# A row transposition for the expert tiles, moved from TensorE to VectorE in 32x32 pieces

## The reference

```
f    = layernorm(x)
rho  = tanh(ctx @ Ws + f @ W + b) . w             # every token against 77 context rows
att  = softmax(masked rho);  t = att @ ctx
x    = x + tanh(g0) * (tanh(t @ Wcw') * f + tanh(t @ Wcb'))
n    = layernorm(x)
top2 of softmax(n @ router')                      # 2 of 8 experts for each token
x    = x + tanh(g1) * sum over experts e of  weight_e * (gelu(n @ w1[e]') @ w2[e]')
```

## Time and profile before

| | us |
|---|---|
| median of three runs | 578.42 |
| the profiled execution | 579.2 |
| its span, first to last instruction | 577.1 |
| PE busy | 518.5 (90%) |
| DVE busy | 355.9 (62%) |
| ACT busy | 354.0 (61%) |
| POOL busy | 112.1 (19%) |

### The profile page before, as it was taken

The page is one execution under the profiler, slowest core; times in us unless marked ns, Lnnn a source line. Parts: engine busy times, 40 slices in busy tenths (PEclk is TensorE's granted clock), DMA queues, the critical chain, the costliest instruction groups (busy, mean ns, idle before and its releaser), DMA issues.

```text
span 577.1 us, 10197 instructions
## 1 busy us (share of the span) xinstructions
PE 518.5 (90%) x3432; PEld 334.1 (58%) x3433; DVE 355.9 (62%) x1176; ACT 354.0 (61%) x314; POOL 112.1 (19%) x96
## 2 busy tenths in 40 slices
PE   7887979667799878989979999999999999999993
PEld 5432323102255434545534555788899999999993
DVE  4889998899984899995799985375111111111110
ACT  1678999989999998999989997231111111111110
POOL 2000000050001161201251111145322122212222
PEclk9688989777899999999999999999999999999998
DMA  4101960045422046233237443359666666665541
GB/s 130 38 0 26 384 257 0 1 151 185 155 76 82 10 152 193 56 120 105 70 109 208 140 136 101 93 155 271 213 184 184 182 182 182 182 182 182 173 98 21
DMA packets 32831, 77.47 MB, mean 134 GB/s; under 512 B 4471, under 2 KB 25591, under 8 KB 26647
## 3 DMA queue, kind: packets, MB, share of 16 engines
q1 hardware_dynamic: 24848, 67.22, 34.2%
q0 software_dynamic: 7344, 9.72, 9.3%
q10 hardware_dynamic: 599, 0.02, 0.1%
HBM read 60.65 MB, written 16.29 MB: 133 GB/s over the span
## 4 chain that ended last, share of the span: by engine, by line
PE 59%; DVE 22%; ACT 13%; DMA 3%; issue 2%; POOL 0%; SPq 0%; DVEq 0%; POOLq 0%
PE h_ps L713 20%; PE y_bank L725 20%; PE rho L678 13%; DVE hbuf L884 11%; ACT hbuf L566 8%; ACT hbuf L572 3%; PE misc L658 3%; PE xsT_bank L667 2%; PE xsT_bank L701 1%; DMA xs<-row_scratch 1%; DMA hgT<-in_x 1%; ACT hgT L595 1%; DMA out<-y_sb,meta 1%; DVE rows L943 1%; DVE stats L851 1%
## 5 line engine op out<-in xcount | busy, mean ns | idle before, releaser
L566 ACT ACTIVATE hbuf<-hbuf 128x2048 f32<-128x2048 f32 (+2 forms) x160 | 247.2, 1593 | 33.0 <-DVE hbuf L884 32.3
L884 DVE TENSOR_SCALAR hbuf<-featT,txtb 128x512 f32<-128x512 f32 x525 | 216.1, 480 | 19.7 <-PE rho L678 18.6
L678 PE MATMUL rho<-hbuf,wpad 128*32 128x512 f32 x1232 | 175.3, 649 | 37.3 <-ACT hbuf L572 26.4
L713 PEld LDWEIGHTS h_ps<-xsT,w_st 128*128 128x128 f32 x1280 | 148.9, 192 | 28.3 <-issue 26.0
L713 PE MATMUL h_ps<-xsT,w_st 128*128 128x128 f32 x1280 | 154.8, 277 | 2.2 <-issue 1.4
L725 PE MATMUL y_bank<-w_sb,hgT 128*128 x640 | 149.7, 384 | 1.7 <-DVE y_sb L1056 1.7
L595 ACT ACTIVATE hgT<-h_ps 128x1024 f32<-128x1024 f32 x40 | 40.7, 1019 | 163.2 <-PE h_ps L713 163.1
L725 PEld LDWEIGHTS y_bank<-w_sb,hgT 128*128 128x128 f32 x640 | 117.4, 190 | 36.3 <-issue 22.5
L510 POOL DMA_INDIRECT out<-y_sb,meta x40 | 66.3, 1657 | 300.1 <-DVE y_sb L1056 160.9
L678 PEld LDWEIGHTS rho<-hbuf,wpad 128*32 128x32 f32 x1232 | 30.1, 113 | 124.2 <-ACT hbuf L572 54.6
L1042 DVE COPY xsT<-xsT_bank 128x256 f32<-128x256 f32 x40 | 16.9, 422 | 81.6 <-PE xsT_bank L701 81.6
(11 more groups left out here) (131 smaller groups left out, 189.4 us busy)
## 6 DMA issues: line engine op xcount, KB each, us to landing
w_st<-in_w SPq DMA_DIRECT2D x40, 1024.0 KB, 4.9
w_sb<-in_w SPq DMA_DIRECT2D x8, 1024.0 KB, 14.0
xs<-row_scratch SPq DMA_DIRECT2D x40, 132.5 KB, 4.7
row_scratch<-pad SPq DMA_DIRECT2D x33, 132.5 KB, 21.6
x_res<-in_x SPq DMA_DIRECT2D x4, 512.0 KB, 5.9
out<-x_res SPq DMA_DIRECT2D x4, 512.0 KB, 3.5
hgT<-in_x SPq DMA_DIRECT2D x3, 512.0 KB, 3.6
out<-y_sb,meta POOLq DMA_INDIRECT x40, 6.3
```

What stands on the lines that cost most here:

```text
L566: ins = s.activation(h, h, ACT.Tanh)
L678: ins = t.matmul(rho[q % 2][32 * j:32 * j + 32, :], wpad[:, c, 31 - r:63 - r], hbuf[:, k % HB, j, :], start=(k == 0), stop=(last and c == ...
L713: ins = t.matmul(h_ps[:, k * P:(k + 1) * P], w1_st[:, par, c, k * P:(k + 1) * P], xsT[:, c, :], start=(c == 0), stop=(c == DC - 1))
L884: ins = v.tensor_scalar(hbuf[:, k % HB, j:j + 1, :], featT[:, c, q:q + 1, :], txtb[:, c, bb, CG * r + j:CG * r + j + 1], None, ALU.add)
```

## The change

From tile 18 on (the 19th) the rows are no longer transposed by TensorE. `xsT` gets two buffers, one for even and one for odd tiles. For these tiles `x_out` waits for the tile's rows (`xs_in`) and until up(i-2) is done with the buffer (`h_ps_ok`), and then issues 16 VectorE transpositions. Each takes 32 partitions (32 rows) and in both halves of 128 columns one group of 32 columns, and writes 32 partitions of `xsT`. The meta operations and their wait follow as before. x_out now runs two tiles ahead: behind y_out(i-1) comes x_out(i+2), where x_out(i+1) stood before y_out(i-1). TensorE's step for these tiles is up(i), down(i-1). Tiles 0 to 17 are transposed as before.

```diff
-        xsT = sb("xsT", [P, DC, P])
+        xsT = sb("xsT", [P, 2, DC, P])
...
-            def step(i, slot4, count, following, turned=None, late=lambda: None):
+            def step(i, slot4, count, turned=None, late=lambda: None):
...
-                if following:
+                if turned:
                     turn_x(i + 1, (slot4 + 1) % 4, turned)
...
+            step(16, 0, 9, 5)
+            for i in range(17, SURE + 1):
+                step(i, i % 4, i // 2 + 1)
             with pe.Fori(0, QUADS) as n:
                 for u in range(1, 5):
-                    step(SURE + u + 4 * n, (SURE + u) % 4, 2 * n + (SURE + u) // 2 + 1, True,
-                         n + (SURE + u + 1) // 4 + 1)
+                    step(SURE + u + 4 * n, (SURE + u) % 4, 2 * n + (SURE + u) // 2 + 1)
...
+            def x_out(i, slot4, count=None):
+                if count is None:
+                    dve.wait_ge(xsT_ps_ok, i + 1)
+                    v.tensor_copy(xsT[:, slot4 % 2].rearrange("p c k -> p (c k)"), xsT_ps).then_inc(xsT_ok, 1)
+                else:
+                    dve.wait_ge(xs_in[slot4], 16 * count)
+                    dve.wait_ge(h_ps_ok, i - 1)
+                    for b in range(0, P, SQ):
+                        for d in range(0, P, SQ):
+                            ins = v.transpose(xsT[d:d + SQ, slot4 % 2, :, b:b + SQ],
+                                              xs[b:b + SQ, slot4, 0:D].rearrange("p (c k) -> p c k", c=DC)[:, :, d:d + SQ])
+                    ins.then_inc(xsT_ok, 1)
...
             x_out(17, 1)
             y_out(15, 3)
-            x_out(18, 2)
+            x_out(18, 2, 5)
             y_out(16, 0)
-            x_out(19, 3)
+            x_out(19, 3, 5)
             y_out(17, 1)
-            x_out(20, 0)
+            x_out(20, 0, 6)
             y_out(18, 2)
+            x_out(21, 1, 6)
             with dve.Fori(0, QUADS) as n:
                 for u in range(1, 5):
-                    x_out(SURE + 1 + u + 4 * n, (SURE + 1 + u) % 4)
                     y_out(SURE - 1 + u + 4 * n, (SURE - 1 + u) % 4)
+                    x_out(SURE + 2 + u + 4 * n, (SURE + 2 + u) % 4, n + (SURE + 2 + u) // 4 + 1)
```

More of the change, by code:

```diff
@@ L334, in flamingo_moe @@
         LOOP_END = SURE + 1 + 4 * QUADS
+        SQ = 32
         block = ctx.enter_context(nc.Block())
@@ L713, in up @@
                         ins = t.matmul(h_ps[:, k * P:(k + 1) * P],
-                                       w1_st[:, par, c, k * P:(k + 1) * P], xsT[:, c, :],
+                                       w1_st[:, par, c, k * P:(k + 1) * P], xsT[:, par, c, :],
                                        start=(c == 0), stop=(c == DC - 1))
@@ L787, in _ @@
             turn_x(14, 2, 4)
[L788 to L791, removed]
+            step(14, 2, 8, 4)
+            step(15, 3, 8, 5, late=lambda: settle("count", NQ - 1))
+            step(16, 0, 9, 5)
+            for i in range(17, SURE + 1):
+                step(i, i % 4, i // 2 + 1)
             with pe.Fori(0, QUADS) as n:
                 for u in range(1, 5):
-                    step(SURE + u + 4 * n, (SURE + u) % 4, 2 * n + (SURE + u) // 2 + 1, True,
-                         n + (SURE + u + 1) // 4 + 1)
+                    step(SURE + u + 4 * n, (SURE + u) % 4, 2 * n + (SURE + u) // 2 + 1)
             for i in range(LOOP_END, NT):
-                step(i, i % 4, i // 2 + 1, i < NT - 1, (i + 1) // 4 + 1)
+                step(i, i % 4, i // 2 + 1)
             e = expert(NT - 1)
@@ L1038, in table @@
                     tlink(v.tensor_tensor(worked[:], worked[:], taken[:, E:2 * E], ALU.add))
-            def x_out(i, slot4):
-                dve.wait_ge(xsT_ps_ok, i + 1)
-                v.tensor_copy(xsT[:].rearrange("p c k -> p (c k)"), xsT_ps).then_inc(xsT_ok, 1)
+            def x_out(i, slot4, count=None):
[10 more added lines that the diff above has]
+                    ins.then_inc(xsT_ok, 1)
                 if not (isinstance(i, int) and i < 4):
@@ L1110, in _ @@
             y_out(15, 3)
-            x_out(18, 2)
+            x_out(18, 2, 5)
             y_out(16, 0)
-            x_out(19, 3)
+            x_out(19, 3, 5)
             y_out(17, 1)
-            x_out(20, 0)
+            x_out(20, 0, 6)
             y_out(18, 2)
+            x_out(21, 1, 6)
             with dve.Fori(0, QUADS) as n:
                 for u in range(1, 5):
-                    x_out(SURE + 1 + u + 4 * n, (SURE + 1 + u) % 4)
                     y_out(SURE - 1 + u + 4 * n, (SURE - 1 + u) % 4)
+                    x_out(SURE + 2 + u + 4 * n, (SURE + 2 + u) % 4, n + (SURE + 2 + u) // 4 + 1)
             for i in range(LOOP_END, NT):
-                if i < NT - 1:
-                    x_out(i + 1, (i + 1) % 4)
                 y_out(i - 1, (i - 1) % 4)
+                if i < NT - 2:
+                    x_out(i + 2, (i + 2) % 4, (i + 2) // 4 + 1)
             y_out(NT - 1, (NT - 1) % 4)
```

## The result

The changed kernel takes 574.37 us (median of 4 runs, 573.49 to 575.17) against 578.62 us for the kernel before on the same chip. The ratio is 0.9919, with a 95% interval of 0.9899 to 0.9940; of 578.62 us that is 4.7 us less, 3.5 to 5.8. The two medians themselves lie 4.25 us apart, inside that interval. The forecast was 574.0 us. A second set of runs of both kernels, taken later, gave 0.9929 (0.9904 to 0.9953).

What follows compares the result with a forecast made beforehand. TensorE's gapless chain, 7.245 us a tile, was taken as the bound. Removing transpositions for 20 tiles (4.35 us) plus 0.1 us at the entry, 4.4 us off 578.42, gave 574.0 us, range 572.3 to 578.0.

Steps and rivals of the forecast that it cites:

- The bound: Steady tiles: TensorE's own work is the chain without a gap; removing a transposition pair saves 0.217 us, 4.35 us for 20.
- rival D: Steady tiles: the 0.22 us only fills a latency between first and second products, so nothing is gained; 578.4 us, chance 0.09.
- The pieces: On VectorE: 16 transpositions per tile at 0.22 us each without overlap, 3.6 us a tile.
- 2.6 us of room: Steady tiles: what is left of 6.2 us after 3.6 us of VectorE transpositions, before TensorE waits.
- Rival C: On VectorE: the transpositions overlap at 0.13 us each, so the entry gives 0.9 us; 573.2 us, chance 0.14.
- The cover of 6.2 us: Steady tiles: time VectorE's transpositions may take before TensorE waits; gone at 0.385 us each.
- VectorE's round: Per tile: y 0.48, 16 transpositions, meta operations 0.41, waits some 0.2 us; passes 7.25 us from 0.385 us a transposition.
- The entry: Start of up(19): at 412.4 against 412.53 us, with VectorE's transpositions on the path; gain 0.1 us.
- the prediction's own sign against this step: At the entry: the step is wrong if up(19) starts more than 0.5 us off 412.4.
- Tile 18's turn: Removing TensorE's transposition of tile 18 gives 0, since up(18) starts when its weights land, at 404.36.
- The adds: Accumulating DMAs follow the weight loads and TensorE, 7.03 us apart; add(37) done 0.8 us before y(38) is out.
- Rival A: The accumulating DMAs keep 7.2 us and become the pace; gain only 2.0 us, 576.4 us, chance 0.16.

Runs made afterwards that it cites:

- one-group run: Changed kernel with its 16 VectorE transpositions per tile all reading and writing partitions 0 to 31, into a buffer nobody reads; 575.82 us.
- 32 pieces: Changed kernel with 32 VectorE transpositions per tile, 16 more than before, into a buffer nobody reads; 616.21 us.
- 24: Changed kernel with 24 VectorE transpositions per tile, 8 more than before, into a buffer nobody reads; 577.67 us.
- one-piece run: Changed kernel with only 1 of the 16 VectorE transpositions per tile, the other 15 left out; 575.05 us.
- run with both transpositions: Kernel before, TensorE's transposition kept, plus 16 VectorE transpositions per tile for tiles 21 to 39 into a buffer nobody reads; ratio 0.9990.

## Why the prediction was right

- *The bound.* That PE's own work is the chain, with no gap in 107.67 us, held: all that left PE's chain left the time, 0.218 us a tile, predicted 0.217, which also rules out rival D. The busy time of a pair, 0.38 us, would have promised 7.6 us in place of 4.4.
- *The pieces.* I took 0.224 us without overlap, 3.6 us a tile. They took 0.236 us each and 0.249 from start to start, 3.97 us a tile. Half of the difference is that a piece is 0.012 us longer than the row it was taken from, half a gap of 0.013 us behind each, which the sum did not have. Together they took 0.4 us of the 2.6 us of room, and 2.3 us were left. Rival C (overlap, 2.1 us a tile) is what the one-group run shows, and is not open to these 16 pieces: each has its own pair of a group read and a group written, so one of the two always changes.
- *Cover and threshold.* The cover of 6.2 us and VectorE's round were right where 32 pieces passed them. With 24 the round came so close that the gaps at the start of the loop's passes cost 1.3 us, which I had not counted.
- *The entry.* Forecast 0.1 us, measured 8.17 - 8.07 = 0.10 us between up(18) and up(19), but that agreement is luck. Counted from the landing of tile 19's rows, up(19) was forecast 412.4 - 408.70 = 3.7 us later; the kernel before took 412.53 - 408.70 = 3.83 us and the changed kernel 413.24 - 409.14 = 4.10 us, in its second profile as well. So from there the step lost 0.27 us, for the pieces were longer than taken. It came out as a gain because the rows landed 3.97 us after up(18) began, where they had landed 4.34 us after it. In the second profile the distance between the two starts of up was 7.62 us, as up(18) then waited 1.81 us for its weights. Read as it stands, the prediction's own sign against this step, up(19) more than 0.5 us off 412.4, is met (413.24 and 413.00); but up(16), ahead of all that changed, began 1.02 and 0.16 us later in these profiles than in that of the kernel before, and less that it is 412.22 and 412.84.
- *Tile 18's turn.* Forecast nothing; up(17) to up(18) is 7.99 against 8.20 us. The wait for the weights is the same, 0.72 us; their load, issued 1.26 us after up(17) began in both kernels, took 6.7 us and not 6.9. In the second profile the same distance was 9.07 us, so this 0.2 us is scatter too.
- *The adds.* Rival A is refuted in both kernels: y never waits for an add in the steady part (2.25 us of wait, and PE ends it), and the adds follow PE. The second profile of the changed kernel has two meta copies behind tile 18's that waited for an add, 1.29 and 1.26 us, and the one-piece run has such a wait at nearly every tile; the period is 7.03 us in both. The 14 intervals between the adds from 432.14 to 530.12 are 7.00 us on average, and at the end add(37) is done before y(38):

```profile
551.07 1.55 POOL L511 DMA_INDIRECT out<-y_sb,meta  x1 [5.49 <-DMA out<-y_sb,meta]
555.62 1.55 POOL L511 DMA_INDIRECT out<-y_sb,meta  x1 [3.00 <-DMA out<-y_sb,meta]
562.31 1.55 POOL L511 DMA_INDIRECT out<-y_sb,meta  x1 [5.14 <-DVE y_sb L1067]
```

- *The sum over the span.* The two profiled spans differ by 3.7 us only, since up(16), which no part of the change reaches, began 1.02 us later in the second (388.89 against 387.87). From there on: 0.21 + 0.10 + 0.15 to up(20), 19 x 0.218 = 4.14 to up(39), 0.1 behind it; 4.7 us together. The start of up(16) scatters: in the later profiles whose edits lie behind it, it was between 386.94 and 388.75 us. In the second profile of the changed kernel the span from up(16) on is 0.46 us longer than in the first (573.0 - 388.03 against 573.4 - 388.89), so that only 4.3 us are left of the 4.7. The 4.14 us of the steady part repeat; what the entry adds does not.

## What to carry to other kernels

Price what you take off the bounding engine by the chain of waits, not by busy time: the pair was 0.38 us busy and 0.22 us of chain. Work that is 18 times dearer on another engine (3.97 against 0.22 us) still pays if it fits between two waits with room to spare; work out that room as a number and the place where the cover begins, since two tiles earlier the same edit lost. Where several waits set a start together, mending one shows the next.

## What the runs showed that was not expected

- Sixteen pieces of 32x64 elements took 3.97 us on VectorE when they change their group of 32 partitions, and 2.12 us when they don't.
- In the run with both transpositions up(18) stood waiting 2.66 us for its weights and then took 5.46 us, not 3.84; the granted clock (third figure from the end, 1.00 is the 2.4 GHz level) was below full speed on average in these stretches, so part of them ran at the 1.2 GHz level:

```profile
404.00:408.00 4.00, 1.92 (x9) 1.92 (x10) 0.00 (x0) 0.00 (x0) 0.00 (x0) 0.76 0.75 283
408.00:412.00 4.00, 4.00 (x29) 3.97 (x29) 1.02 (x5) 0.41 (x1) 1.57 (x1) 0.81 0.83 219
```

A wait at the entry can thus cost 1.6 us more than its length. The one-group run has the same, 5.46 us behind a wait of 2.02 us. In the changed kernel, where the wait was 0.72 and 1.81 us in its two profiles, up(18) took 3.84 us.
- An accumulating DMA took 4.7 us from its issue to the next one's where no weight load ran beside it (562.31 to 567.01) and about 7 us beside one.
